# Attention scores at four row positions, the output projection in a score bank, and no copy of the output

## The reference, cut to what is computed

```
h0  = x + Wo(softmax(min(Q K^T / 4, mask)) V) + bo      with Q = Wq LN(x) + bq, K, V from the context
h   = xn + aw(LN1(xn))         with xn = LN(h0), LN1 with gains and offsets
t   = LN2(h);  logits = gate_w t;  two best experts, softmax weights
out = h0 + h + sum over the two experts of weight * down(silu(gate t) * up t)
```

## Time and profile before

| | us |
|---|---|
| median of 3 runs | 621.02 |
| lowest, highest | 617.53, 622.01 |
| profiled execution | 620.13 |
| its span in the profile | 618.6 |

### The profile page before, as it was taken

One profiled execution on the slowest core, in us unless ns is written; L12 is line 12 of the kernel. 1 busy time (PEld: TensorE's weight loads), 2 busy tenths in 40 slices (PEclk: granted clock), 3 DMA queues, 4 the chain that ended last, 5 costly groups with the idle time before them and its releaser, 6 DMA issues.

```text
span 618.6 us, 13662 instructions
## 1 busy us (share of the span) xinstructions
PE 527.6 (85%) x3197; PEld 452.7 (73%) x3198; DVE 345.9 (56%) x876; ACT 281.4 (45%) x701; POOL 287.2 (46%) x374
## 2 busy tenths in 40 slices
PE   2579999999997513899999998999999999999960
PEld 1357788888886302788888887888888888888850
DVE  1846788788876474466434345836536534365330
ACT  1177878787874141534323325434335323353210
POOL 4321436455545455357633416756554644345120
PEclk9779999999998555999999999899999999999995
DMA  8870010101010044011312375171262222612123
GB/s 217 217 314 0 19 36 18 35 17 34 17 35 27 27 86 161 10 28 27 44 26 34 77 211 178 17 200 55 43 187 59 34 43 28 179 55 34 17 23 143
DMA packets 27088, 46.57 MB, mean 75 GB/s; under 512 B 9718, under 2 KB 22544, under 8 KB 26768
## 3 DMA queue, kind: packets, MB, share of 16 engines
q1 hardware_dynamic: 15312, 35.77, 17.8%
q0 software_dynamic: 9088, 9.52, 9.7%
q10 hardware_dynamic: 2656, 0.91, 0.9%
HBM read 36.67 MB, written 11.61 MB: 78 GB/s over the span
## 4 chain that ended last, share of the span: by engine, by line
PE 65%; ACT 12%; DMA 7%; DVE 4%; issue 3%; POOL 1%; ACTq 0%; POOLq 0%; SPq 0%; DVEq 0%
PE psum L1168 15%; PE psum L1169 15%; PE psum L1170 15%; ACT p_sb L646 9%; PE psum L1100 6%; DMA w_raw<-in_experts 6%; PE psum L1199 4%; PE psum L1048 4%; PE psum L1043 2%; PE psum L1208 1%; ACT qT L611 1%; ACT uT L635 1%; PE psum L1055 1%; ACT rows L640 1%; PE psum L1064 1%
## 5 line engine op out<-in xcount | busy, mean ns | idle before, releaser
L1168 PE MATMUL psum<-w_hi,tb_hi 128*128 x288 | 117.9, 409 | 5.1 <-DVE tb_lo L1004 4.2
L1169 PE MATMUL psum<-w_lo,tb_hi 128*128 x288 | 113.7, 395 | 0.0
L1170 PE MATMUL psum<-w_hi,tb_lo 128*128 x288 | 113.7, 395 | 0.0
L1168 PE MATMUL psum<-w_hi,aT_hi 128*128 x288 | 85.0, 295 | 4.3 <-DVE aT_lo L992 4.3
L1169 PE MATMUL psum<-w_lo,aT_hi 128*128 x288 | 82.1, 285 | 0.0
L1170 PE MATMUL psum<-w_hi,aT_lo 128*128 x288 | 82.1, 285 | 0.0
L992 DVE TENSOR_TENSOR aT_lo<-psum,aT_hi 128x512 fp32r<-128x512 f32 x72 | 46.4, 685 | 63.0 <-ACT aT_hi L678 63.0
L674 ACT ACTIVATE silu<-psum 128x512 f32<-128x512 f32 x36 | 21.6, 600 | 117.4 <-PE psum L1170 117.4
L570 POOL DMA_INDIRECT acc_rows<-o_sb,add_at x36 | 58.6, 1629 | 34.1 <-POOL add_at L568 32.9
L998 DVE TENSOR_TENSOR act<-psum,silu 128x512 f32<-128x512 f32 x72 | 49.3, 686 | 33.8 <-PE psum L1170 28.5
L1168 PEld LDWEIGHTS psum<-w_hi,tb_hi 128*128 128x128 f32 x288 | 54.9, 191 | 16.9 <-issue 7.3
(11 more groups left out here) (170 smaller groups left out, 1029.5 us busy)
## 6 DMA issues: line engine op xcount, KB each, us to landing
w_raw<-in_experts SPq DMA_DIRECT2D x24, 768.0 KB, 4.4
w_raw<-in_experts SPq DMA_DIRECT2D x2, 3072.0 KB, 14.0
x_sb<-in_x SPq DMA_DIRECT2D x8, 256.0 KB, 5.8
z_rows<-rows SPq DMA_DIRECT2D x16, 128.0 KB, 1.7
acc_rows<-x_sb SPq DMA_DIRECT2D x16, 128.0 KB
ceil_f<-in_mask ACTq DMA_DIRECT2D x2, 308.0 KB, 11.6
blk<-lists POOLq DMA_DIRECT2D x36, 1.0 KB
rows<-z_rows,gather_at POOLq DMA_INDIRECT x36, 2.9
```

Of the source, the lines that this page charges most:

```text
L1168: nc.tensor.matmul(dst, hi, weights(w_hi, slot, at, cols), start=first, stop=False)
L1169: nc.tensor.matmul(dst, hi, weights(w_lo, slot, at, cols), start=False, stop=False)
L1170: return nc.tensor.matmul(dst, lo, weights(w_hi, slot, at, cols), start=False, stop=last)
```

## The change

- **Scores.** The columns of Q and K are reordered on the host (through the rows of Wq, bq, Wk, bk) so that the heads 4g to 4g+3 lie in the rows 32g to 32g+31 of both halves. The products of one half take 32 rows, hold 2 heads (154 columns), and stand at the row positions 0, 32, 64 and 96 of the array, each writing its own bank 0 to 3. There are 8 of them instead of 4. k_diag has 2 column blocks instead of 8 per half. The first score add now reads banks 0 and 1 (8 heads, semaphore s_ps), the second banks 2 and 3 (8 heads, semaphore s2_ps); before it was 12 heads and 4.
- **Projection.** Transposes of o and the output projection move from bank 7 to bank 3 (OUT_BANK), the weighted values and logits from bank 3 to bank 7 (VALUE_BANK). In TensorE's step the transposes of o move from behind the scores to behind the logits and wait, besides for o, until both score adds of the same step are done; the projection moves behind the aw product. ScalarE's copy oT moves behind uT.
- **Output.** acc_rows is the output itself, with 128 rows more for padding; the tokens are numbered batch by batch; the copy at the end is gone.
- **Table.** Expert 0 gets at least two blocks (`least`), one more block may stand behind the usual ones (BLOCKS), and the numbers by which the splitting of the next expert's weights is placed are moved by one.

The diff, cut to its core:

```diff
+ROW_TILES = 4
+BANK_HEADS = HEADS // ROW_TILES
+PAIR = BANK_HEADS // KD
-FULL_BANKS = HEADS // BANK_HEADS
+FULL_BANKS = ROW_TILES // 2
+OUT_BANK, VALUE_BANK = 3, 7
-BLOCKS = FULL_BLOCKS + EXPERTS - 1
+BLOCKS = FULL_BLOCKS + EXPERTS
...
-        acc_rows = nc.dram_tensor("acc_rows", (TOKENS + P, D), F32).ap()
+        acc_rows = out
...
             sp.wait_ge(added, every)
-            for b in range(BATCH):
-                sp.dma_start(out_tiles[:, b], acc_tiles[:, b]).then_inc(out_done, 16)
-            sp.wait_ge(out_done, 16 * BATCH)
+            sp.sem_inc(out_done, 1)
...
-                    nc.vector.tensor_tensor(of(x1_sb, t5), bank[7][:, 0:D], of(x1_sb, t5), ALU.add).then_inc(x1_done, 1)
+                    nc.vector.tensor_tensor(of(x1_sb, t5), bank[OUT_BANK][:, 0:D], of(x1_sb, t5), ALU.add).then_inc(x1_done, 1)
...
-                    dve.wait_ge(s_ps, 2 * number(t2) + 1)
+                    dve.wait_ge(s_ps, FULL_BANKS * (number(t2) + 1))
...
-                    dve.wait_ge(s_ps, 2 * number(t2) + 2)
+                    dve.wait_ge(s2_ps, (ROW_TILES - FULL_BANKS) * (number(t2) + 1))
...
-                for q in range(HALF_HEADS):
+                for q in range(PAIR):
...
-            step(nc.vector.tensor_scalar(nblk[:, :], nblk[:, :], 1.0, None, ALU.max))
+            step(nc.vector.tensor_tensor(nblk[:, :], nblk[:, :], least[:, :], ALU.max))
...
-                if within(t4, TILES):
-                    pe.wait_ge(o_done, number(t4) + 1)
-                    wait_count(pe, x1_done, number(t4))
-                    transposed(bank[7], o_sb[:, t4[1], :]).then_inc(oT_ps, 1)
+                    if within(t5, TILES):
+                        pe.wait_ge(x1_done, number(t5) + 1)
+                    for m in range(KD):
+                        for g in range(ROW_TILES):
+                            g0, at = g * (P // ROW_TILES), m * PAIR * KEYS
+                            last = nc.tensor.matmul(
+                                bank[g][:, at:at + PAIR * KEYS], qT[g0:g0 + P // ROW_TILES, par, m, :],
+                                k_diag[g0:g0 + P // ROW_TILES, par, m, :, :].rearrange("p q k -> p (q k)"),
+                                start=True, stop=True, tile_position=(g0, 0))
+                            if m == KD - 1:
+                                last.then_inc(s_ps if g < FULL_BANKS else s2_ps, 1)
...
-                if within(t4, TILES):
-                    pe.wait_ge(oT_done, number(t4) + 1)
-                    row_product(bank[7][:, 0:D], oT[:, t4[1], :, :], wo_sb).then_inc(wo_ps, 1)
...
+                if within(t4, TILES):
+                    pe.wait_ge(o_done, number(t4) + 1)
+                    wait_count(pe, x1_done, number(t4))
+                    if within(t2, TILES):
+                        pe.wait_ge(s_done, 2 * number(t2) + 2)
+                    transposed(bank[OUT_BANK], o_sb[:, t4[1], :]).then_inc(oT_ps, 1)
...
+                if within(t4, TILES):
+                    pe.wait_ge(oT_done, number(t4) + 1)
+                    row_product(bank[OUT_BANK][:, 0:D], oT[:, t4[1], :, :], wo_sb).then_inc(wo_ps, 1)
```

More of the change, by code:

```diff
@@ L232, in xattn_moe @@
         numbers = sb("numbers", [1, EXPERTS])
+        least = sb("least", [1, EXPERTS])
         next_f = sb("next_f", [1, J])
@@ L264, in xattn_moe @@
         x_sb = tile_sb("x_sb", [P, TILES, D])
-        k_diag = tile_sb("k_diag", [P, BATCH, KD, HALF_HEADS, KEYS])
+        k_diag = tile_sb("k_diag", [P, BATCH, KD, PAIR, KEYS])
         ceil_f = tile_sb("ceil_f", [P, TILES, KEYS])
@@ L307, in xattn_moe @@
         sh_done = sem("sh_done")
+        s2_ps = sem("s2_ps")
         bq_done = sem("bq_done")
@@ L618, in tiles @@
                     nc.scalar.activation(e2[:, t7[1], :], gap[:, t7[1], :], ACT.Exp).then_inc(e2_done, 1)
-                if within(t4, TILES):
-                    act_e.wait_ge(oT_ps, number(t4) + 1)
-                    nc.scalar.activation(oT[:, t4[1], :, :], bank[7][:, 0:D], ACT.Copy).then_inc(oT_done, 1)
                 if within(t1, TILES):
@@ L636, in tiles @@
                                              bias=vecs[:, b1_c, k:k + 1], scale=vecs[:, g1_c, k:k + 1]).then_inc(uT_done, 1)
+                if within(t4, TILES):
+                    act_e.wait_ge(oT_ps, number(t4) + 1)
+                    nc.scalar.activation(oT[:, t4[1], :, :], bank[OUT_BANK][:, 0:D], ACT.Copy).then_inc(oT_done, 1)
                 if within(t0, TILES):
@@ L887, in _ @@
             nc.vector.tensor_scalar(numbers[:, :], expert_f[0:1, :], 1.0, None, ALU.add).then_inc(router_const, 1)
+            nc.vector.tensor_scalar(least[:, :], expert_f[0:1, :], 1.0, 1.0, ALU.is_lt, ALU.add).then_inc(router_const, 1)
             dve.wait_ge(v_in, 32)
@@ L1063, in weighted_values @@
                         first, heads = chunk_heads(c)
-                        done = nc.tensor.matmul(bank[3][:, first * VW:(first + heads) * VW], pT[0:w, t3[1], c, :],
+                        done = nc.tensor.matmul(bank[VALUE_BANK][:, first * VW:(first + heads) * VW], pT[0:w, t3[1], c, :],
                                                 v_chunks[0:w, c, t3[1], 0:heads, :].rearrange("p s v -> p (s v)"),
@@ L1131, in tiles @@
                         pe.wait_ge(topi_done, number(t7) + 1)
-                    transposed(bank[3], z2[:, t6[1], :]).then_inc(tT_ps, 1)
-                if within(t4, TILES):
-                    pe.wait_ge(oT_done, number(t4) + 1)
-                    row_product(bank[7][:, 0:D], oT[:, t4[1], :, :], wo_sb).then_inc(wo_ps, 1)
+                    transposed(bank[VALUE_BANK], z2[:, t6[1], :]).then_inc(tT_ps, 1)
                 if within(t5, TILES):
@@ L1237 @@
     down = a["L0_ffn_down_proj"].reshape(EXPERTS, D, IC, P).transpose(0, 3, 2, 1).reshape(EXPERTS, P, IC * D)
+    heads = (np.arange(ROW_TILES)[None, :, None] * BANK_HEADS + np.arange(KD)[:, None, None] * PAIR + np.arange(PAIR)[None, None, :]).reshape(-1)
+    by_rows = (heads[:, None] * HD + np.arange(HD)[None, :]).reshape(-1)
+    for n in ("Wq", "bq", "Wk", "bk"):
+        a["L0_xattn_" + n] = a["L0_xattn_" + n][by_rows]
     laid = {
```

67 lines of the change are left out of this document (28 added, 39 removed).

## The result

The changed kernel takes 675.55 us (median of 4 runs, 674.44 to 677.8) against 621.51 us for the kernel before in the same session (4 runs): a ratio of 1.088, 95% interval 1.083 to 1.093. The forecast was 626.7 us with a range of 617 to 637, so it was wrong by 49 us. The profiled execution of the changed kernel has a span of 673.3 us against 618.6, which is 54.7 us more.

What follows compares the result with a forecast made beforehand. Attention was taken as paced by a ring of scores, small TensorE items, ScalarE's exponentials and qT. Terms -12.5 - 2.3 + 13.5 + 7.0 = +5.7 us on the 621.02 median gave 626.7 us, range 617 to 637.

Steps and rivals of the forecast that it cites:

- The ring: Steady attention step: late projection closes a chain between TensorE and VectorE, 11.5 us a turn against 10.3, +13.5 us.
- The clock: Steady attention steps: the turn of 11.5 us was summed from TensorE items at full clock.
- Rival 1: Attention steps: TensorE's wait for `chosen` halves its clock, about +1.0 us per hit step; 631 to 636 us, chance 0.2.
- The scores: Attention score products: 1.8 us instead of 2.34, bounds 0.6 and 2.34; gain not seen from tile 4 on.
- rival 2: Score products: no overlap, drains between tiling modes, 2.34 us or more; 629.5 us, chance 0.15.
- The wait: Steady step: o's transposes wait for both score adds, 2.35 us from first add's start to second's end.
- The drain: Attention steps after the last scores: later projection add and two longer steps, +7.0 us (bounds +5 and +8.5).
- The end: Closing output copy vanishes with its issuing and waiting, nothing else late behind it: -12.5 us.
- The start: Up to tile 4's first score add: tile 1 -2.6 us, with later tiles -2.3 in sum.
- k_diag: Start of kernel: four writes instead of sixteen, but VectorE waits for v_flat instead: 0 us.
- edits at nothing: Token order, `least`, the added block and s2_ps, in table stage and behind the last block: 0 us.

Runs made afterwards that it cites:

- Experiments 5 and 6: The changed kernel with useless identity transposes filling TensorE's pauses (four versions, last 644.53 us); the changed kernel with the wo product moved ahead of aw (660.2 us).
- experiment 2: Kernel before without the output copy, plus the moved, late projection and its wait for the second score add, old scores kept: 661.54 us, ratio 1.063.
- third kernel of experiment 5: The changed kernel with 15 identity transposes behind the scores and none elsewhere: 663.91 us, ratio 1.071.
- Experiment 3: Kernel with old scores, no copy and late projection, without TensorE's wait for the second score add: 640.93 us, ratio 1.034, against 661.54 with that wait.
- experiment 1: Kernel before with only the output copy removed, accumulating straight into the output: 609.87 us, ratio 0.981.

## Why the prediction was wrong

**The ring: right.** The two turns that are at full clock throughout take 11.5 and 11.7 us, with VectorE's wait of 1.83 us where the forecast put 1.8. Experiments 5 and 6 show its members: fill the pauses and it is 11.66 us, take aw out of it and it is 10.67. What the forecast called +13.5 us is 14 to 17.

**The clock: the step that failed.** The forecast added up its turn at the full clock, and the clock fell: 0.74 between 76 and 169 us. Rival 1 named that mechanism ("TensorE ... waits some 2 us for `chosen`"; it waited 1.89), and the forecast gave it 0.2 and a price of "about +1.0 us in a step that is hit". It was not only that wait: the clock fell with the old scores too, where the wait for `chosen` was 0.4 to 0.8 us (experiment 2), and with the wait filled (the third kernel of experiment 5). The price is the larger error, since rival 1's own 631 to 636 us is 40 us short as well.

I had charged the half level to aw alone; but the ring contains, one behind the other, o's transposes, half the values, aw and wo, all on TensorE, and also waits for gw. From first score add to add of the projection it takes 9.40 us at the half level and 5.85 at the full: +3.55 us in a hit turn (0.65 until o's transposes, these 0.18, values 0.96, aw 0.90, wo 0.86). The forecast read the values as paced by weight loads and charged them nothing; at the half level their ten records take 2.01 us until aw starts instead of 1.05, so those slow down as well.

Nor is it only the steady steps: from tile 1 to tile 4 the kernel lost 10.4 us where I had -1.1 and +1.4, so that the -3.6 at tile 1 became +6.8 at tile 4, in place of the forecast's -2.3; the clock from the first score add to that of tile 4 was 0.59, against 0.91 before. Of the 48.9 us between forecast and trace 28.6 stand in the stretch, 9.1 ahead of it, 5.6 in the drain, 3.6 at the end and 2.0 in table and experts.

And the chance: rival 1 set one pause beside one stretch of the kernel before, and I did not work out TensorE's busy share in the new turn. TensorE goes from 89.6 busy us in 93 to 78.2, since the ring's half on VectorE lasts longer than what TensorE has to do beside it: from the add at 122.24 us its items end near 125.9, and it waits until 127.76. The ring by itself already said that: 11.5 us a turn for the work that had filled 10.3, with shorter scores besides. The forecast had both numbers and did not put them together.

**The scores: overlap, and a loss.** I took 1.8 us with bounds of 0.6 and 2.34; it is 0.81. The Trainium skill ("TensorEngine Tiling (Array Packing)", Overview and Key Properties) promises up to four times for 32 rows; the trace shows 2.34 to 0.81, 2.9 times. The next product of all 128 rows starts 0.74 us behind the first of the sixteen where nothing holds it up (114.45 and 115.19 us), so rival 2, without overlap and with drains between, is out. "Whatever is won in the scores is not seen from tile 4 on" was right for the ring and wrong for the total: from experiment 2 to the changed kernel, scores, k_diag and the table's small edits being the difference, it costs 14.0 us (from the copy of the counts on, both take 390 us). At full clock the turn is no longer than in experiment 2 (the shortest 11.5 against 11.6), so what is lost in the stretch goes with the clock, 0.74 against 0.87.

**The wait.** The forecast knew the wait for the second score add as the first term of the ring and charged its length. Experiment 3 gives 18 to 20.6 us for it. The delay itself, 0.33 us in the turn shown, makes by my estimate some 5 us of that in 15 steps; with the rest the clock recovers from 0.87 to 0.94.

**The drain: +12.6 us instead of +7.0** (bound +8.5). The mechanism was right, the size off. Most of it runs at the half level; the forecast knew that for the wo products alone, but it holds for the whole chain. From the last first score add to the copy of the counts, in the changed kernel and in the one before:

```profile
229.81:282.80 52.99, 32.57 (x137) 26.41 (x137) 26.17 (x122) 14.84 (x46) 21.37 (x33) 0.60 0.08 26
```

```profile
180.93:221.30 40.37, 25.95 (x139) 20.62 (x137) 24.68 (x122) 14.50 (x46) 20.95 (x33) 0.70 0.10 31
```

This term is known to some 3 us only: the same instructions took 37.4 us in experiment 1 at a clock of 0.79. VectorE's adds of the projection there, in the kernel after:

```profile
237.94 0.42 DVE L741 TENSOR_TENSOR x_sb<-psum,x_sb 128x256 f32<-128x256 f32 x1 [4.54 <-PE psum L1052]
...
252.62 0.42 DVE L741 TENSOR_TENSOR x_sb<-psum,x_sb 128x256 f32<-128x256 f32 x1 [7.22 <-PE psum L1052]
...
264.69 0.42 DVE L741 TENSOR_TENSOR x_sb<-psum,x_sb 128x256 f32<-128x256 f32 x1 [4.89 <-PE psum L1052]
```

The first comes 8.1 us behind the last first score add (3.5 before, where the forecast took 4.2), the next 14.7 and 12.1 us later (8.4 and 8.5 before).

**The end: -8.9 us instead of -12.5.** "Nothing else is late behind it" was false: GpSimd's drain of 7.6 us ran under the copy. The chain of waits showed only the copy; the instructions of the closing line would have shown the drain in the trace of before.

**The start, k_diag, edits at nothing: right within 1 to 2 us.** VectorE's first scores come at 28.46 us (29.43 before), tile 1's 7.82 us later (10.44 before, the -2.6 of the forecast), its idle time ahead of v_chunks is 4.57 us, and table and experts moved by 2.0 us together.

With the terms as measured the sum is 6.8 + 42.1 + 12.6 + 0.6 + 1.4 - 8.9 = 54.6 us, the difference of the spans within 0.1.

What is not settled: whether the pause behind the scores would lower the clock by itself. The third kernel of experiment 5 had nearly only the one ahead of gw, and its clock fell; filling both held it; no kernel had only the other.

## What to carry to other kernels

Before an edit that makes TensorE wait once a step, add up its busy time per turn of the new chain; if its share of the turn falls, price the whole chain at the half clock, with every TensorE item in it, weight-load-bound ones too, and compare that with the gain. Shortening an item of TensorE that is off the chain can cost time, since what it leaves is a pause. When a closing transfer is removed, look at each engine's last instruction for what ran beneath it.

## What the runs showed of the hardware

- Products of 32 rows at four row positions into four banks: sixteen records in 0.81 us, against eight full ones in 2.34 us for the same 1232 columns. At two row positions, 64 rows: twelve records in 1.31 us.
- Useless work made the kernel faster: fifteen identity transposes a step (2.1 us together) took the changed kernel from 675.55 to 644.53 us.
- Removing a wait that left TensorE idle 0.2 to 0.6 us in a turn gave 18 to 20.6 us over the kernel, with a clock that fell four times in eleven turns instead of eight.
- The half level slows small products whose weight loads pace them as much as large ones: ten records of values 2.01 us instead of 1.05 until the next product, aw 2.04 instead of 1.09.
- GpSimd's drain behind the last indirect transfer lasts 5.8 to 7.6 us in the thirteen kernels and ends the execution where nothing longer follows.
